# Four-layer transformer on one core: expert tiles ordered by row blocks, sums and norms of two batches beside the tiles, expert rows turned back from columns

## The reference

```python
xn = _modulate(_ln(x), sh_mlp, sc_mlp)
xf = xn.reshape(-1, C)
gate_logits = xf @ w_gate
topk_logits, topk_idx = jax.lax.top_k(gate_logits, TOP_K)          # TOP_K = 2 of 4 experts
gates = jax.nn.softmax(topk_logits, axis=-1)
cw = jnp.sum(jax.nn.one_hot(topk_idx, NUM_EXPERTS, dtype=xf.dtype) * gates[..., None], axis=1)
hmid = jax.nn.gelu(jnp.einsum('tc,ech->eth', xf, w1) + b1[:, None, :], approximate=True)
eo = jnp.einsum('eth,ehc->etc', hmid, w2) + b2[:, None, :]
moe = jnp.einsum('te,etc->tc', cw, eo).reshape(B, N, C)
return x + g_mlp[:, None, :] * moe
```

## Time and profile before

| | |
|---|---|
| time, median of 3 runs (lowest to highest) | 1857.52 us (1854.61 to 1862.54) |
| profiled execution: its own time, its span | 1856.44 us, 1854.7 us |
| mean granted clock of PE | 0.927 of full speed |
| busy: PE, DVE, ACT, POOL | 1569.1 us (85%), 1390.3 (75%), 875.6 (47%), 718.3 (39%) |
| chain that ended last: PE, DVE, ACT, POOL | 53%, 27%, 2%, 0% of the span |
| layer 0's front, tile loop, layer 1's qkv | about 328 to 451 us, 451 to 896 us, 942 to 1012 us |

### The profile page before, as it was taken

The page is one execution under the profiler, slowest core; times in us unless marked ns, Lnnn a source line. Parts: engine busy times, 40 slices in busy tenths (PEclk is TensorE's granted clock), DMA queues, the critical chain, the costliest instruction groups (busy, mean ns, idle before and its releaser), DMA issues.

```text
span 1854.7 us, 29296 instructions
## 1 busy us (share of the span) xinstructions
PE 1569.1 (85%) x9005; PEld 1012.3 (55%) x9005; DVE 1390.3 (75%) x2684; ACT 875.6 (47%) x1714; POOL 718.3 (39%) x1595
## 2 busy tenths in 40 slices
PE   6889998643988896998178999988989899988999
PEld 4632223522877885887155222357877322248885
DVE  7787785564899885764687888776898888867763
ACT  4557775211433442332044777752355477773222
POOL 0565600136576672003466665666666400000000
PEclk9999999765989998998579999999999999999999
DMA  6566656115644534313435333421114422400001
GB/s 170 135 187 133 147 139 149 45 63 161 176 121 108 143 94 150 97 49 98 109 74 164 76 77 77 104 40 5 18 5 121 134 77 77 114 26 1 1 1 51
DMA packets 132935, 172.24 MB, mean 93 GB/s; under 512 B 32066, under 2 KB 113972, under 8 KB 132681
## 3 DMA queue, kind: packets, MB, share of 16 engines
q1 hardware_dynamic: 127178, 156.02, 29.0%
q0 software_dynamic: 5632, 14.70, 7.0%
HBM read 116.59 MB, written 49.67 MB: 90 GB/s over the span
## 4 chain that ended last, share of the span: by engine, by line
PE 53%; DVE 27%; SPq 6%; issue 5%; DMA 5%; ACT 2%; another core or an unknown queue 1%; POOL 0%; DVEq 0%; ACTq 0%
PE psum L1240 16%; PE psum L1383 7%; PE psum L1372 7%; PE psum L1358 6%; PE psum L1531 5%; PE psum L1615 4%; DVE minus_max L1928 3%; DMA k_stack<-qk_parts_d 2%; DVE bn L1836 2%; PE psum L1640 1%; SPq L711 1%; PE psum L1297 1%; SPq L751 1%; SPq L712 1%
## 5 line engine op out<-in xcount | busy, mean ns | idle before, releaser
L1928 DVE TENSOR_REDUCE minus_max<-psum 128x2 bf16<-128x1024 f32 x384 | 452.4, 1218 | 88.2 <-PE psum L1358 81.0
L1138 ACT ACTIVATE probs<-psum 128x512 f32<-128x512 f32 x768 | 418.7, 601 | 168.0 <-PE psum L1372 165.7
L1372 PE MATMUL psum<-q_stack,k_stack 109*128 109x512 bf16 x768 | 261.0, 387 | 13.2 <-DMA q_stack<-minus_max_t 5.9
L1240 PE MATMUL psum<-x_split,w_hi 128*128 128x512 f32 x684 | 257.9, 418 | 13.2 <-DVE x_tail L1875 4.8
L1358 PE MATMUL psum<-k_stack,q_stack 108*128 108x512 bf16 x720 | 219.9, 387 | 20.6 <-DVE minus_max L1928 9.8
L865 POOL TENSOR_TENSOR qr_m<-qr_m 64x8 f32<-64x8 f32 (+35 forms) x544 | 198.9, 366 | 42.6
L1372 PEld LDWEIGHTS psum<-q_stack,k_stack 109*128 109x128 bf16 x768 | 72.6, 97 | 249.6 <-ACT probs L1138 178.9
L1383 PE MATMUL psum<-probs,v_stage 128*32 128x512 f32 x1536 | 204.3, 605 | 1.2 <-ACT o_t L1127 1.1
L1240 PEld LDWEIGHTS psum<-x_split,w_hi 128*128 128x128 f32 x684 | 133.6, 195 | 41.9 <-issue 10.5
L1065 ACT ACTIVATE hid_f<-psum 128x512 f32<-128x512 f32 x99 | 59.3, 599 | 196.9 <-PE psum L1240 168.7
L1531 PE MATMUL psum<-w_hi,hid_hi 128*128 128x288 f32 x396 | 122.2, 309 | 33.3 <-DVE branch L2172 21.6
(11 more groups left out here) (334 smaller groups left out, 3393.9 us busy)
## 6 DMA issues: line engine op xcount, KB each, us to landing
qk_parts_d<-qk_parts SPq DMA_DIRECT2D x36, 384.0 KB, 4.4
moe_rows_d<-skew_upper SPq DMA_DIRECT2D x16, 836.0 KB, 7.9
raw_b<-in_L_cond_w SPq DMA_DIRECT2D x30, 432.0 KB, 3.4
raw_a<-in_L_cond_w SPq DMA_DIRECT2D x30, 384.0 KB
q_stack<-qk_parts_d SPq DMA_DIRECT2D x48, 216.0 KB
k_stack<-qk_parts_d SPq DMA_DIRECT2D x48, 216.0 KB
tile_rows<-moe_rows_d SPq DMA_DIRECT2D x11, 704.0 KB, 4.5
q_stack<-qk_parts_d SPq DMA_DIRECT2D x48, 144.0 KB
```

Source lines behind the costliest of these rows:

```text
L1138: act.activation(PE_[:, v // 4, v % 4, :], psum[:, score_bank(v), :], ACT.Exp, scale=SCALE).then_inc(s_e, 1)
L1240: i = pe.matmul(dst, a, r, start=(n == 0), stop=(n == len(terms) - 1))
L1372: pe.matmul(psum[:, score_bank(v), :], K6[0:STK + 1, g % 4, h, P * kt:P * kt + P], Q6[0:STK + 1, g % 4, h, :], start=True, stop=True).then ...
L1928: dve.tensor_reduce(MX[:, g % 2, 2 * u:2 * u + 2], psum[:, o:o + 2, :], AX.X, ALU.max, negate=True).then_inc(s_mx, 1)
```

## The change

- **Tile order.** The table lists the tiles by block of 512 rows within each expert's list: block 0 of experts 0 to 3, then block 1, and so on. Batch b's rows stand in its experts' first b + 1 blocks, so the results of batch 0 are complete after 4 tiles, of batch 1 after 8 (READY). `row_places` translates the places of rows.
- **Sums in the loop.** POOL gathers batch 0 after 7 more reflectors and one, batch 1 after 7 and one again; DVE sums them at units 49, 57, 82 and 88 and makes layer 1's norm of batches 0 and 1 at units 60 and 92; batch 0 is turned at units 94 and 95. Batches 2 and 3 are gathered once tile 10 is stored and summed within layer 1's qkv of batch 1.
- **Rows from columns.** DVE makes only the statistics; POOL makes the reciprocal root with a power (`scale_of_rows`), ACT the normed rows (`norm_x`); the modulation is applied by ACT on the turned columns (`mod_x`), from columns loaded once (`load_mlp_cols`); PE turns the modulated columns back to rows (`turn_back`), ACT copies them to the scatter's source (`rows_x`). Rows in HBM have 288 floats; DVE makes the tails after loading (`tile_tails`). The front has 20 steps.
- **Loop.** The hidden block's high part is made by ACT (`hidden_hi`) instead of DVE; weights are split in thirds; tile 0 is turned into three banks; tile 0's rows are fetched ahead of tile 1's weights; skew entries from unit 4, placed 21 rows each in tiles 4, 5 and 6; the exponential from unit 64.
- **Clearing.** The 16 clearing DMAs are issued by ACT, behind the fifth exponential of each group.

```diff
-SKEW_UNIT, EXPM_UNIT = 9, 66
+SKEW_UNIT, EXPM_UNIT = 4, 64
-FRONT = 11 + 2 * FRONT_SKEW
-PIVOTS = (0, 12, 28, 64)
+FRONT = 12 + 2 * FRONT_SKEW
+PIVOTS = (0, 12, 19, 20, 27, 28, 64)
+READY = (4, 8, TILES, TILES)
+COMBINE_UNIT = {5 * HM + 4: (0, 0), 6 * HM + 3: (1, 0), 9 * HM + 1: (0, 1), 9 * HM + 7: (1, 1)}
+NORM_UNIT = {6 * HM + 6: 0, 10 * HM + 2: 1}
+TURN_UNIT = 10 * HM + 4
...
+            if t + 1 < TILES and m in (2, 5, 8):
+                return [("1m", t + 1, m // 3)]
+            if t + 1 < TILES and m in (4, 7):
+                return [("2m", t + 1, (m - 4) // 3)]
+            if t >= 1 and m == 1:
+                return [("2m", t, 2)]
+            return []
...
                 sp.wait_ge(s_tb, 1)
                 e = tile_expert(1)
+                sp.wait_ge(s_sd, 32 * 16)
+                load_rows(0)
+                load_tile_w1(1, 0, e)
+                load_rows(1)
                 load_tile_b2(1, e)
...
-                    if t == 5:
+                    if t == 4:
                         sp.wait_ge(s_vc, 1)
...
-                        place_skew(range(0, 31))
-                    if t == 6:
-                        place_skew(range(31, D3 - 1))
+                    if 4 <= t <= 6:
+                        place_skew(range(21 * (t - 4), 21 * (t - 3)))
...
+            def scale_of_rows(b):
+
+                tiles = slice(TT * b, TT * b + TT)
+                gp.wait_ge(s_bn, b)
+                gp.tensor_scalar(RST[:, tiles], MV[:, tiles, 1], LN_EPS, None, ALU.add).then_inc(s_rs, 1)
+                gp.wait_ge(s_rs, 4 * b - 3)
+                gp.tensor_tensor(RST[:, tiles], RST[:, tiles], MHF[:, :].to_broadcast([P, TT]), ALU.pow).then_inc(s_rs, 1)
+                gp.tensor_scalar(MV[:, tiles, 0], MV[:, tiles, 0], -1.0, None, ALU.mult).then_inc(s_rs, 1)
+                gp.wait_ge(s_rs, 4 * b - 1)
+                gp.tensor_tensor(MV[:, tiles, 0], MV[:, tiles, 0], RST[:, tiles], ALU.mult).then_inc(s_rs, 1)
...
             def gather(k, b):
-                if k == 1:
-                    gp.wait_ge(s_cb, b + 1)
+                gp.wait_ge(m_y, 16 * READY[b])
+                if b < 2 and k + 2 * b >= 1:
+                    gp.wait_ge(s_cb, k + 2 * b)
+                if b >= 2:
+                    gp.wait_ge(s_cb, 4)
...
+            reflectors(PIVOTS[1], PIVOTS[2])
             gp.wait_ge(s_iy, 1)
-            for b in range(B):
-                gather(0, b)
-            gp.wait_ge(m_y, 16 * TILES)
-            for b in range(B):
-                gather(1, b)
-            for k in range(PIVOTS[2], PIVOTS[3]):
-                reflector(k)
+            gather(0, 0)
+            reflectors(PIVOTS[2], PIVOTS[3])
+            gather(1, 0)
+            reflectors(PIVOTS[3], PIVOTS[4])
+            gather(0, 1)
+            reflectors(PIVOTS[4], PIVOTS[5])
+            gather(1, 1)
+            for b in (2, 3):
+                for k in range(2):
+                    gather(k, b)
+            reflectors(PIVOTS[5], PIVOTS[6])
...
+            def norm_x(b):
+                act.wait_ge(s_rs, 4 * b)
+                for t in range(TT):
+                    i = TT * b + t
+                    a = act.activation(XMR[b][:, t, :], XR[:, i, :], ACT.Identity, bias=MV[:, i, 0:1], scale=RST[:, i:i + 1])
+                a.then_inc(s_xm, 1)
...
+            def rows_x(b):
+                for c in range(KC + 1):
+                    n = P if c < KC else TAIL
+                    act.wait_ge(s_xb, 3 * b + c + 1)
+                    act.activation(XMR[b][:, :, P * c:P * c + n], psum[:, 4 + c, 0:TT * n].rearrange("p (t n) -> p t n", t=TT), ACT.Copy).then_inc(s_xc, 1)
...
+                act.wait_ge(m_g, j + 1)
+                act.activation(HH[:, m % 3, :], HF[:, j % 2, :], ACT.Copy).then_inc(m_hh, 1)
...
                     act.activation(PE_[:, v // 4, v % 4, :], psum[:, score_bank(v), :], ACT.Exp, scale=SCALE).then_inc(s_e, 1)
+                    if v == 4 and l == 0:
+                        clear_rows(B - 1 if first else bb, HG - 1 if first else g - 1)
...
+            def turn_back(b):
+
+                if b == 0:
+                    pe.wait_ge(s_ot, B * HG)
+                for c in range(KC + 1):
+                    n = P if c < KC else TAIL
+                    for t in range(TT):
+                        i = pe.transpose(psum[:, 4 + c, n * t:n * t + n], FX[0:n, c, P * t:P * t + P], IDN[0:n, 0:n])
+                    i.then_inc(s_xb, 1)
...
-                        elif k == 8:
+                        elif k == 9:
                             logits(b)
-                        elif k == 9:
+                            turn_back(b)
                             turn_logits(b)
...
+            def row_places():
+
+                shape = [P, NT * 2, 15]
...
+            def tile_tails(t):
+                dve.wait_ge(m_x[t % 2], 16 * (t // 2 + 1))
+                for r in range(2):
+                    i = dve.tensor_copy(XROW[t % 2][:, :, C + TAIL * r:C + TAIL * (r + 1)], XROW[t % 2][:, :, KC * P:C])
+                i.then_inc(m_xt, 1)
...
-                link(dve.tensor_copy(HH[:, m % 3, :], HF[:, j % 2, :]))
                 dve.tensor_tensor(HL[:, m % 3, :], HF[:, j % 2, :], HH[:, m % 3, :].bitcast(F32), ALU.subtract).then_inc(m_h, 1)
...
                 gate_weights()
+                row_places()
+                tile_tails(0)
+                for c in range(KC + 1):
+                    tile_low(0, c)
...
+                    if j in COMBINE_UNIT:
+                        combine(*COMBINE_UNIT[j])
+                    if j in NORM_UNIT:
+                        stats(NORM_UNIT[j], 1, 0)
+                        normalise(1, 0, NORM_UNIT[j])
...
+                    low(l, 0, 1)
+                    qkv(l, 0)
+                    combine(0, 2)
                     combine(1, 2)
                     stats(2, l, 0)
-                    low(l, 0, 1)
-                    qkv(l, 0, lambda m: normalise(l, 0, 2) if m == KC else None)
-                    combine(1, 3)
-                    stats(3, l, 0)
+                    normalise(l, 0, 2)
+                    qkv(l, 1, fourth_batch)
                     low(l, 0, 2)
                     normalise(l, 0, 3)
-                    qkv(l, 1)
-                    low(l, 0, 3)
-                    qkv(l, 2)
+                    qkv(l, 2, lambda m: low(l, 0, 3) if m == QN - 1 else None)
```

More of the change, by code:

```diff
@@ L316, in build @@
         s_b2 = [sem(f"b2_loaded{i}") for i in range(2)]
-        s_sh = [sem(f"mlp_rows_loaded{i}") for i in range(2)]
+        s_mq = sem("mlp_cols_loaded")
+        s_bn = sem("statistics_made")
+        s_rs = sem("rstd_steps")
+        s_xb = sem("moe_rows_turned_back")
+        s_xc = sem("moe_rows_placed")
         s_cn = sem("route_constants_made")
@@ L367, in build @@
         LOAD = 16 * 2 * len(PART_RUNS)
+        MLP_COLS = 16 * (KC + 1)
         def tn(l, s, b):
@@ L377, in chunk_bank @@
         def chunk_bank(n, c):
+            if n < 2 * B and n >= B + 1:
+                return (2, 3, 0)[c]
             return c if place_in(n) == 4 or (n >= 2 * B and place_in(n) == 5) else (2, 3, 2)[c]
@@ L583, in load_gate, with load_mlp_cols @@
                 sp.dma_start((GMSA, GMLP)[g][:, :, :], GD[l][2 + 3 * g].partition_broadcast(P)).then_inc((s_gm, s_gl)[g], 16)
-            def load_mlp_rows(b):
-                if b >= 2:
-                    sp.wait_ge(s_xm, b - 1)
-                sp.dma_start(SHS[b % 2][:, :, :], GD[0][3:5, b, :].partition_broadcast(P)).then_inc(s_sh[b % 2], 16)
+            def load_mlp_cols():
+                sp.wait_ge(s_gd, mods_stored(0))
+                src = GD[0][3:5]
+                dst = MODC[:, 0, :, 2:4, :].rearrange("p c v b -> p c (v b)")
+                with nc.allow_non_contiguous_dma("columns of the modulation"):
+                    for c in range(KC + 1):
+                        rows = P if c < KC else TAIL
+                        sp.dma_start(dst[0:rows, c, :], src[:, :, P * c:P * c + rows].rearrange("v b p -> p (v b)")).then_inc(s_mq, 16)
             def tile_rows(t):
@@ L1104, in qk_parts @@
                         turned(l, 0, 3, (m,))
+                    if l == 1 and b == 2 and m >= 3:
+                        turned(l, 0, 3, (0, 1) if m == 3 else (2,))
                     if m == QN - 1 and b < B - 1:
@@ L1127, in o_t, with clear_rows @@
                 act.activation(OT[:, bass.ds(i, 1), :].rearrange("p o n -> p (o n)"), bk(6), ACT.Copy).then_inc(s_ot, 1)
+            def clear_rows(bb, g):
+                rows = XSD.rearrange("(o r) c -> o (r c)", o=B)[bass.ds(bb, 1), :].rearrange("o (p a n) -> (o p) a n", p=D3, a=D3)
+                n = MOE_ROWS * C // (B * D3 * D3)
+                zeros = UO[:, :, :].rearrange("p b d -> p (b d)")[:, 0:n].unsqueeze(1).to_broadcast([D3, D3 // 4, n])
+                act.dma_start(rows[:, D3 // 4 * g:D3 // 4 * (g + 1), :], zeros).then_inc(s_zr, 16)
             def attention(l, bb, g, first=False):
                 i = 4 * bb + g
```

(21 more changed lines are left out.)

361 lines of the change are left out of this document (183 added, 178 removed).

## The result

The changed kernel takes 1836.42 us (median of 4 runs, 1825.07 to 1838.72) against 1858.15 for the kernel before in the same set of runs: ratio 0.9867, 95% interval 0.9827 to 0.9906. It is shorter, as forecast, but by 22 us (1.3%) instead of 84, and outside the range. The profiled execution took 1825.07 us, its span is 1823.3, 31.4 less than before.

A forecast was written before the change was run, and what follows sets the result against it. PE and DVE, handing work to each other, were taken to bound the kernel, with three stretches mostly waiting. Terms −5 −6 −8 −37 −28 = −84 from 1856.4 gave 1772 us, own range 1750 to 1790, wider range 1728 to 1812.

The forecast's parts named there:

- Clearing on ACT's queue: Layer 0's attention: zeros leave SP's queue and rows narrow, so SP reaches the next maxima earlier; −5 us.
- Rival 1: Layer 0's attention: generating zeros blocks ACT as long as SP was busy issuing, some 25 us lost in 16 groups; 1802.
- The front: Front of the experts: DVE loses 6.3 us a batch, but PE gets more transposes; −6 us, bounds −14 and +3.
- The start of the loop: Last slots to first hidden block's split: rows fetched earlier, turned into three banks, 29.5 us instead of 37.8; −8 us.
- The loop: Tile loop: cast to ACT, splits in thirds, shorter exponential wait and tile 10, less added sums and norms; together −37 us.
- Tiles 1 to 4: Tile loop: DVE falls under 31 us a tile, so PE is the bound; from 147.3 us, −23 us.
- Exponential: Tile loop: wait for the placed skew entries 9 us rather than 12.2, units around it recover too; −4 us.
- Tile 10: Last tile with the exponential's last steps, last products and copies: 40 us instead of 60.5; −20 us.
- rival 3: Tile loop: POOL late, DVE stands at the sum of unit 82 or 88; 29 us lost, 1801; 14%.
- Layer 1's qkv: Last copy to layer 1's attention: batches 0 and 1 already normed, 88 us instead of 115.6; −28 us.
- Rival 2: Ping-pong and waits shorten more than counted: front −14, attention −11, placing hidden −12, qkv −38; 1734; 22%.
- Rival 4: Tile loop: gelu and copy in series on ACT lengthen every unit; at 1.2 us a unit 1892; 4%.

The follow-up runs named there:

- e5: Changed kernel, zeros still on ACT's queue but in runs of 836 B on a longer buffer instead of 684 B: 1807.31 us.
- e1: Changed kernel with the zeros issued by SP again, behind the stack loads of their group: 1789.67 us, ratio 0.9637 to the kernel before.
- e4: Changed kernel with the zeros issued by SP, ahead of the stack loads of their group: 1818.40 us.
- e8: e1 with skew entries from unit 9 instead of 4 and placings of 28, 28 and 7 instead of 21 each: 1776.38 us, ratio 0.9562.
- e3: Kernel before with only its zeros moved to ACT, behind exponential 4 of each group: 1879.14 us, ratio 1.0115.
- f2: e11 run again, beside the changed kernel (608 B runs, zeros on ACT's queue): ratio 0.9653 to the kernel before.
- f3: f2 with the same runs of zeros 16 B further on in memory: ratio 0.9769 to the kernel before.
- e11: Changed kernel, zeros on ACT's queue, the same bytes in runs of 608 B instead of 684 B: 1785.93 us, kernel before 1841.41 there.
- f1: Changed kernel run again without edits, in a later set of runs: ratio 0.9854 to the kernel before.
- e10: Changed kernel, zeros on ACT's queue, the same bytes in runs of 912 B instead of 684 B: 1794.60 us, kernel before 1841.41 there.
- e12: Changed kernel, zeros on ACT's queue in 684 B runs, neighbouring runs from neighbouring partitions: 1795.68 us, kernel before 1841.41 there.

## Why the prediction was wrong, step by step

**The step that failed** is "Clearing on ACT's queue": I took −5 with bounds of −11 and +8, and it was +41.6. Both bounds were priced from what the engines that issue have to do, SP's pace and ACT's 1.2 us. What the transfers do to each other had no price at all, nor had the lower clock that PE gets behind a wait. What the runs showed in its place: zeros in the DMA engines beside or ahead of the stacks' loads make PE wait 33 us longer, and the clock adds some 12. The windows of the kernel before had the warning, which I didn't read: in 121 to 290 us of its attention the share of the DMA engines is 0.66, against 0.14 in the front.

```profile
121.00:290.00 169.00, 158.58 (x863) 46.11 (x861) 134.22 (x137) 123.56 (x230) 71.69 (x194) 0.99 0.66 156
```

The order of SP's queue was what kept the zeros out of the stacks' way; the change took away an order, not an issue. I also took the narrower rows for 18% less work. They weren't: a run of 684 B took as much of an engine as one of 836 B (e5: 3.6% x 16 x 1805.6 us / 16640 = 62 ns; changed: 61 ns), the zeros landed later and the stacks were held up further. With that one step undone (e1) the kernel takes 1789.67 us; of the 18 us left to 1772, 8 are that the step's gain didn't come either (the last copy came at 329.9 against 327.2), and the others lie in the terms below. That 1789.67 touches my own range of 1750 to 1790 confirms the rest of the sum only as a whole: errors in it cancel.

**Rival 1**, ACT held by its own DMA, saw a loss in the right place (some 30 us, 1802 in all) but by another mechanism: ACT computes again 0.75 us after each issue, and e4 loses the time without ACT. The Trainium skill's "DMA: Bandwidth & Descriptors", section "Issuing engines are not separate DMA queues", says that another issuing engine saves only the sequencer's time. The runs agree that nothing else is saved, and add what I didn't draw from it: the order within one queue is lost, at 40 us here (e1 against the changed kernel).

**The front**, −6, was −1.9. DVE lost 19 us of work, as counted, and the period stayed: windows show PE at 56 us of 93 with 25% more matmuls (402 against 322). That the added transposes took the gain is argued, no run took them away.

**The start of the loop**, −8, was −10.7: the rows are fetched at once behind the scatter and turned into three banks; how much each of these gave wasn't separated.

**The loop**, −37, was −35.1, with errors that cancel. Tiles 1 to 4: −23 forecast, −21.1, but the cast gave only 9 of it. Tile 0: +4 and +4.4, though half of it or more is the loads of skew weights (4.9 us of waiting, 6.1 back in e8), which I hadn't seen. Exponential: −4, but tiles 6 and 7 became 4.2 us longer (87.5 to 91.7), with the wait still 11.7 us, since the last 21 placings were issued until 730.5. Tile 10: −20, was −24.9, and that was luck in part. I read DVE's 12.5 us of standing as the wait for the first sum's gather. The line shown is the last step of the matrix exponential, and the first sum, at 874.12, waits for nothing:

```profile
874.12 1.80 DVE L2180 SCALAR_TENSOR_TENSOR moe_y<-moe_y,logits,gate_mlp 128x288 f32<-128x288 f32 x4
```

In 857 to 870 us of the kernel before PE makes only 17 matmuls, with pauses that the trace puts down to issue, and DVE and ACT stand, while POOL issues its gathers; e3 shows the same hole (12.5 us). In the changed kernel, where no gather stands in tile 10, it is gone. Why it was there stays open. The sums waited for nothing, so rival 3 did not happen.

**Layer 1's qkv**, −28, was −22.6. The first two sums began 14.2 and 19.4 us behind the last take, where 14.6 and 19.6 were worked out. The whole took 94.6 us against 88. Of these 6.6 us 1.6 are a matter of where the stage ends (before, it is 117.2 us here and was 115.6 in the sum); the others lie in the splitting and turning behind the sums.

Rival 2 fell, since neither the attention nor the front nor layer 1's qkv shortened by more than the forecast; the clock did rise there, as it said (0.68 to 0.76, 0.56 to 0.81). Rival 4 fell by the pace of 31 to 32 us a tile.

## What to carry to other kernels

A DMA moved to another engine's queue loses its place in the order; before moving one, read the DMA share of the stage and ask which load it used to stand behind. If it must run beside loads that somebody waits for, cut it into runs that begin and end on multiples of 32 B (f2 against f3, 21.5 us), or issue it behind them (e1). Fewer bytes were no gain here, where the number of runs stayed. And a wait of PE can be dearer than its own length: here PE came back at half the clock for 5 us behind one of 4.8 us, so count what follows it too.

## What the runs showed of the hardware

- A DMA write to memory costs by its runs: 608 B took 44 to 45 ns of an engine when each began and ended on a multiple of 32 B (e11, f2), 54 ns when all were 16 B further on (f3), 684 B 61 to 63 ns (changed, f1), 836 B 61 to 62 ns (e3, e5), 912 B 60 ns (e10).
- Of runs alike in size and number (684 B), another order of the addresses took 54 instead of 61 ns (e12, one execution; the kernel before was 0.9% faster in that set of runs).
- SP's issue of a stack's load gets longer beside the zeros: 2.33 us instead of 0.76 with the zeros on ACT's queue, and 1.75 instead of 0.77 or 0.81 behind zeros in SP's own queue (e4, at 206.07 us).
- Behind a wait of 4.77 us PE ran at a granted clock of 0.50 for 5 us, and two matmuls took 1.03 to 1.06 us instead of 0.59 to 0.60.
